# Values between keys and queries, the residual in quarters, inputs normalised a unit sooner, GpSimd's two copies swapped

## The reference, cut to what matters

```
xn = layernorm(x)
# branch 1: causal linear attention, 16 heads of 64
Q = elu(xn @ Wq + bq) + 1;  K = elu(xn @ Wk + bk) + 1;  V = xn @ Wv + bv
KV_t = KV_(t-1) + k_t v_t^T;  Ks_t = Ks_(t-1) + k_t
o_t = (q_t KV_t) / (q_t . Ks_t + 1e-6);      attn = o @ Wo + bo
# branch 2: soft decision tree of depth 8
gate = sigmoid((xn @ tree_Wq^T) @ routers^T)           # 255 nodes
leaf_prob = product of gate or 1 - gate along each path # 256 leaves
tree = (leaf_prob @ leaf_values) @ Wout_w^T + Wout_b
out = x + attn + tree
```

## Time and profile before

| | us |
|---|---|
| median of 3 runs | 1218.85 |
| lowest, highest | 1218.16, 1219.29 |
| profiled execution | 1219.74 |
| its span, first to last instruction | 1218.0 |
| PE busy | 1161.8 (95%) |
| DVE busy | 836.1 (69%) |
| POOL busy | 804.3 (66%) |
| ACT busy | 681.0 (56%) |

### The profile page before, as it was taken

How to read it: one execution, slowest core, us unless ns; L and a number is a source line. 1 busy time by engine, 2 the same in 40 slices (tenths; PEclk the granted TensorE clock), 3 DMA queues, 4 the chain that set the end, 5 groups by cost and what they waited for, 6 DMA issues and landing times.

```text
span 1218.0 us, 48108 instructions
## 1 busy us (share of the span) xinstructions
PE 1161.8 (95%) x21233; PEld 996.0 (82%) x21233; DVE 836.1 (69%) x2186; ACT 681.0 (56%) x990; POOL 804.3 (66%) x951
## 2 busy tenths in 40 slices
PE   5899999999999999999999999999999999999986
PEld 4789788887878879778897888878788797888866
DVE  4775875858677585876858667585876758767482
ACT  3563674737557374673737547374673746647371
POOL 3586667667666676766667676676666667676571
PEclk9999999999999999999999999999999999999998
DMA  7143532525344252533524435252452625335251
GB/s 233 20 80 52 86 68 54 91 52 89 60 65 90 45 97 50 89 63 55 93 49 90 58 62 98 45 89 54 84 68 57 94 45 89 63 57 77 55 71 36
DMA packets 271298, 87.54 MB, mean 72 GB/s; under 512 B 250721, under 2 KB 269424, under 8 KB 271088
## 3 DMA queue, kind: packets, MB, share of 16 engines
q1 hardware_dynamic: 271088, 84.46, 39.0%
HBM read 14.43 MB, written 8.39 MB: 19 GB/s over the span
## 4 chain that ended last, share of the span: by engine, by line
PE 63%; DVE 18%; ACT 6%; DMA 5%; issue 4%; POOL 3%; SPq 1%; POOLq 0%; ACTq 0%; DVEq 0%
PE w_pair L811 17%; PE s_pair L811 11%; PE s_pair L826 9%; PE o_pair L826 9%; PE s_pair L893 5%; PE o_pair L947 4%; DVE snaps L732 4%; DVE qT L659 3%; PE o_pair L933 3%; DVE oT L697 3%; DVE v_aug L668 3%; DVE xn L645 2%; DMA k_turned<-k_planes 2%; PE kv_pair L906 2%; ACT ex L522 2%
## 5 line engine op out<-in xcount | busy, mean ns | idle before, releaser
L406 POOL TENSOR_SCALAR_AFFINE_SELECT aT<-aT 64x512 f32<-64x512 f32 x256 | 171.7, 671 | 264.6 <-ACT aT L562 254.9
L562 ACT ACTIVATE aT<-s_pair 128x512 f32<-128x512 f32 x128 | 76.5, 598 | 382.6 <-PE s_pair L893 382.6
L811 PE MATMUL w_pair<-xnT,wk 128*128 128x512 f32 x768 | 212.1, 411 | 2.2 <-ACT k_tok L535 2.2
L811 PE MATMUL s_pair<-xnT,wq 128*128 128x512 f32 x756 | 201.1, 401 | 0.6 <-DVE o_tok L709 0.3
L732 DVE TENSOR_TENSOR snaps<-kv_pair,snaps 128x65 f32<-128x65 f32 x768 | 173.4, 226 | 26.4
L467 POOL COPY k_tok<-k_turned 128x1024 uint16<-128x1024 uint16 x126 | 171.4, 1361 | 22.7 <-POOL ffn_tok L459 14.6
L811 PE MATMUL w_pair<-wv,xnT 128*128 128x512 f32 x654 | 170.0, 395 | 0.0
L525 ACT ACTIVATE ex<-ex 128x512 f32<-128x512 f32 x256 | 161.9, 633 | 8.1
L449 POOL COPY k_planes<-kT 128x1024 uint16<-128x1024 uint16 x126 | 132.7, 1053 | 49.2 <-issue 26.5
L811 PEld LDWEIGHTS w_pair<-xnT,wk 128*128 128x128 f32 x768 | 134.3, 188 | 34.4 <-ACT k_tok L535 2.7
L811 PEld LDWEIGHTS s_pair<-xnT,wq 128*128 128x128 f32 x756 | 135.1, 188 | 27.0 <-DVE o_tok L709 2.4
(11 more groups left out here) (117 smaller groups left out, 2076.6 us busy)
## 6 DMA issues: line engine op xcount, KB each, us to landing
x_in<-in_L_attn_x_dram SPq DMA_DIRECT2D x16, 256.0 KB, 3.1
x_in<-in_L_attn_x_dram SPq DMA_DIRECT2D x32, 128.0 KB, 3.2
out_dram<-y_buf SPq DMA_DIRECT2D x32, 128.0 KB, 1.7
out_dram<-y_buf SPq DMA_DIRECT2D x64, 64.0 KB, 2.3
k_turned<-k_planes SPq DMA_TRANSPOSE x126, 3.2
stage<-in_L_attn_Wv_dram SPq DMA_DIRECT2D x2, 512.0 KB, 7.8
stage<-in_L_attn_Wk_dram SPq DMA_DIRECT2D x2, 512.0 KB, 10.0
stage<-in_L_attn_Wq_dram SPq DMA_DIRECT2D x2, 512.0 KB, 12.2
```

The costliest lines, as they stand in the source:

```text
L406: pool.affine_select(out=part, in_=part, compare_op=ALU.is_ge, fill=0.0, base=0, pattern=[[0, 2 * CH], [1, D]], channel_multiplier=-1).the ...
L811: last = pe.matmul(dst, l, r, start=i == 0, stop=i == len(steps) - 1)
```

## The change: what it does

- **Fills.** In units 1 to 6 the V product becomes the head, between K and Q, and xT, leaf or gate becomes the tail, after Q. Unit 0 (V1 twice) and unit 7 stay. `values_first` is gone.
- **GpSimd.** The keys of unit n+2 are put together before the output of unit n is taken apart. The residual is added in four quarters of 128x256, in units 1, 3, 4 and 5. The inverse deviation of block g+2 is computed among the tree levels of unit 7 of block g.
- **Normalising.** Block g+2 is normalised on DVE in unit 7 of block g, right behind its statistics, instead of in unit 0 of block g+1.
- **Turned output.** The high part (ACT) comes right after K's passes, the low part (DVE, L697) after K and V and before Q, instead of last or after Q.
- **SP.** The block is loaded in unit 6 instead of unit 2.
- **PE's waits.** The waits for mask, norm, inputs and leaves move into the middle or before the last matmul of the fills.

```diff
--- before.py
+++ after.py
@@ -42,19 +42,20 @@
     keys = divmod(n + 3, PAIRS) if n + 3 < blocks * PAIRS else None
     queries = divmod(n + 2, PAIRS) if n + 2 < blocks * PAIRS else None
     more = g + 1 < blocks
+
     head, tail = [], []
     if p == 0:
         head, tail = [("V1", 0, g)], [("V1", 1, g)]
     if p in (1, 2):
-        tail = [("V1", p + 1, g)]
+        head = [("V1", p + 1, g)]
         if more:
-            head = [("xT", p - 1, g + 1)]
+            tail = [("xT", p - 1, g + 1)]
+    if 3 <= p < PAIRS - 1 and more:
+        head = [("V0", p - 3, g + 1)]
     if p in (3, 4):
-        head = [("leaf", p - 3, g)]
-        if more:
-            tail = [("V0", p - 3, g + 1)]
+        tail = [("leaf", p - 3, g)]
     if p in (5, 6) and more:
-        head, tail = [("gate", p - 5, g + 1)], [("V0", p - 3, g + 1)]
+        tail = [("gate", p - 5, g + 1)]
 
 
     fills = [(("K", keys[1], keys[0]), W0)] if keys else []
@@ -363,8 +364,8 @@
                     turn_output(n)
                 if n + 3 < UNITS:
                     turn_keys(n + 3)
-                if p == 2 and g + 2 < BLOCKS:
-                    sp.wait_ge(x_consumed, g + 1)
+                if p == 6 and g + 2 < BLOCKS:
+                    sp.wait_ge(x_consumed, CH * (g + 1))
                     load_block(g + 2)
             store(BLOCKS - 1)
             sp.wait_ge(y_stored, STORES * BLOCKS)
@@ -407,13 +408,12 @@
                                        pattern=[[0, 2 * CH], [1, D]], channel_multiplier=-1).then_inc(a_masked, 1)
                 pool.wait_ge(a_masked, 2 * n + 2)
 
-            def residual(g):
+            def residual(g, c):
                 if g:
                     pool.wait_ge(y_stored, STORES * g)
                 pool.wait_ge(x_loaded[g % 2], LOADS * (g // 2 + 1))
-                pool.tensor_tensor(y_buf[:, :, :], x_in[:, g % 2],
-                                   y_bias[:, 0].unsqueeze(1).to_broadcast([P, CH, hid]), ALU.add)\
-                    .then_inc(x_consumed, 1)
+                pool.tensor_tensor(y_buf[:, c], x_in[:, g % 2, c], y_bias[:, 0], ALU.add).then_inc(x_consumed, 1)
+                pool.wait_ge(x_consumed, CH * g + c + 1)
 
             def gates(g):
                 for i in range(2):
@@ -438,6 +438,7 @@
                 pool.wait_ge(leaf_step, g * LEVEL_STEPS + 2 * l + 2)
                 pool.tensor_tensor(left, src[:, :, 0:n], right, ALU.subtract).then_inc(leaf_step, 1)
 
+            RESIDUAL_AT = (1, 3, 4, 5)
             FIRST_LEVELS = {0: range(0, 5), 1: range(5, 7), 2: range(7, depth)}
 
             def take_apart(m):
@@ -477,20 +478,19 @@
             take_apart(2)
             for n in range(UNITS):
                 g, p = divmod(n, PAIRS)
-                if p == 0 and g + 1 < BLOCKS:
-                    inverse_deviation(g + 1)
-                    pool.wait_ge(rstd_ready, 2 * g + 4)
+                if n == 0:
+                    inverse_deviation(1)
+                    pool.wait_ge(rstd_ready, 4)
                 if n + 1 < UNITS:
                     mask(n + 1)
+                if n + 2 < UNITS:
+                    put_together(n + 2)
                 if by_dma(n):
                     take_output_apart(n)
-                if n + 2 < UNITS:
-                    put_together(n + 2)
                 if n + 3 < UNITS:
                     take_apart(n + 3)
-                if p == 1:
-                    residual(g)
-                    pool.wait_ge(x_consumed, g + 1)
+                if p in RESIDUAL_AT:
+                    residual(g, RESIDUAL_AT.index(p))
                 if n in FIRST_LEVELS:
                     for l in FIRST_LEVELS[n]:
                         level(l, 0)
@@ -500,6 +500,10 @@
 
                     pool.wait_ge(o_turned_in, 16 * units_by_dma(n))
                     for l in range(depth):
+                        if l == 4 and g + 2 < BLOCKS:
+
+                            inverse_deviation(g + 2)
+                            pool.wait_ge(rstd_ready, 2 * g + 6)
                         level(l, g + 1)
                     pool.wait_ge(leaf_step, (g + 2) * LEVEL_STEPS)
 
@@ -605,15 +609,12 @@
                     put_output_together(n - 1)
                 for name, _ in unit_fills(n // PAIRS, n % PAIRS, BLOCKS):
                     kind, i, g = name
+                    if turned and kind != "K":
+                        high_of_turned(n - 1)
+                        turned = False
                     if kind in "KQ":
                         exponential(name)
-                        if kind == "Q" and turned:
-                            high_of_turned(n - 1)
-                            turned = False
                     elif kind == "oT":
-                        if turned:
-                            high_of_turned(n - 1)
-                            turned = False
                         high_of_output(name)
                     elif kind == "xT":
                         high(name, xnT[:, g % 2, 0, i])
@@ -641,6 +642,9 @@
                 if g == 1:
 
                     dve.wait_ge(filled[bank_of["tree", 1, 0]], count_of["tree", 1, 0])
+                if g > 1:
+
+                    dve.wait_ge(o_whole, units_by_dma((g - 1) * PAIRS - 2))
                 for c in range(CH):
                     last = dve.tensor_scalar(xn[:, c], x_in[:, g % 2, c], mean_var[:, c, 0:1], rstd[:, c:c + 1],
                                              ALU.subtract, ALU.mult)
@@ -669,14 +673,6 @@
                                   bv_all[:, half * n:(half + 1) * n].rearrange("p (h e) -> p h e", e=D), ALU.add)\
                    .then_inc(drained[bank_of[name]], 1)
 
-            def values_first(fills, p):
-
-                if p not in (2, PAIRS - 2):
-                    return fills
-                return [f for f in fills if f[0] not in ("Q", "V0", "V1", "oT", "kT")] + \
-                    [f for f in fills if f[0] in ("V0", "V1")] + \
-                    [f for f in fills if f[0] in ("Q", "oT", "kT")]
-
             def low_of_output(name):
                 _, p, g = name
                 dve.wait_ge(oT_hi, g * PAIRS + p + 1)
@@ -685,7 +681,7 @@
 
             def output(name):
                 i = name[1]
-                dve.wait_ge(x_consumed, name[2] + 1)
+                dve.wait_ge(x_consumed, CH * (name[2] + 1))
                 dve.wait_ge(filled[bank_of[name]], count_of[name])
                 dve.tensor_tensor(y_buf[:, 2 * i:2 * i + 2], psum_of(name).rearrange("p (c d) -> p c d", d=hid),
                                   y_buf[:, 2 * i:2 * i + 2], ALU.add)\
@@ -767,21 +763,21 @@
                 norm(n)
                 if n + 1 < UNITS:
                     carry(n + 1)
-                if p == 0 and g + 1 < BLOCKS:
-                    normalise(g + 1)
-                fills = [name for name, _ in unit_fills(g, p, BLOCKS)]
+                if n == 0:
+                    normalise(1)
                 turned = n and by_dma(n - 1)
-                for name in values_first(fills, p):
+                for name, _ in unit_fills(g, p, BLOCKS):
                     kind, i, b = name
+                    if turned and kind not in ("K", "V0", "V1"):
+                        low_of_turned(n - 1)
+                        turned = False
                     if kind in "KQ":
                         phi(name)
                     elif kind == "oT":
-                        if turned:
-                            low_of_turned(n - 1)
-                            turned = False
                         low_of_output(name)
                         if p == PAIRS - 1 and g + 2 < BLOCKS:
                             layer_norm(g + 2)
+                            normalise(g + 2)
                     elif kind in ("V0", "V1"):
                         values(name)
                     elif kind == "xT":
@@ -1051,13 +1049,18 @@
                 def normed():
                     until(o_normed, n + 1)
 
-                def head_ready():
-
+                def tail_ready():
                     for kind, i, g in (f for f, _ in fills):
                         if kind == "xT":
                             until(xn_ready, g + 1)
-                        if kind == "leaf" and i == 0:
+                        if kind == "leaf":
                             until(leaf_step, (g + 1) * LEVEL_STEPS)
+
+                def inputs_ready():
+                    for kind, i, g in (f for f, _ in fills):
+                        if kind == "V0" and i == 0:
+                            for t in range(KT_):
+                                until_drained(("xT", t, g))
 
                 def masked():
                     if n + 1 < UNITS:
@@ -1069,18 +1072,20 @@
                         until(s_copied, n + 2)
                     if kind in ("oT", "y"):
                         normed()
-                    if kind == "V0" and i == 0:
-                        for t in range(KT_):
-                            until_drained(("xT", t, g))
                     if kind == "leaf":
 
```

(23 more changed lines are left out.)

## The result

The changed kernel takes 1270.12 us (median of 4, 1263.3 to 1271.33) against 1218.57 for the kernel before (4 runs): a ratio of 1.0411, 95% interval 1.0373 to 1.0448. I had forecast 1234.5 and 1217 to 1244: the direction is right, the size is three times too small.

The account below looks back on a forecast made before the run. PE, busy 95%, was taken as the bound, so the change could only move its waits. Blocks of 74.39 against 73.375 gave +14.2 over 14, ends +1.5: +15.7, median 1234.5 us (+1.3%), range 1217 to 1244.

Parts of the forecast that it names:

- The floor of 7.71: Intervals p=1 to 6: scores to first ACT pass over Q 5.53, then 2.18 to next scores, at least 7.71 us.
- the floor I gave (73.73): Lowest block time forecast, all six intervals at 7.71 or 7.77 us: 73.73 us a block, 1225 us in total.
- the 74.39 of the forecast: New block: 19.55 for p=7, 7.80 for p=0, six intervals of 7.84; against 73.375 before, +1.015 us.
- The race of L697 and keys apart: DVE's L697 probably held by GpSimd's copy, two chances in three; qT 0.2 us late, intervals 7.90, taken as 7.84.
- The removed waits: PE waits that go: 0.6 us at p=0, 1.3 at p=2, 0.5 at p=6, at most 0.88 in some p=7.
- the 42 I gave as all that could be won: PE's waits inside the blocks, 3.0 us a block in the mean over 14 blocks: 42 us.
- Normalising, inverse deviation and block load in p=7: Work moved to or wanted in p=7, put at no cost: DVE idles 6.27 us there, the unit has 19.5.
- Rival 4: Move to p=7 is late; PE waits there 0.5 to 1 us a block: 1242 to 1249, chance 0.05.
- rival 3: L697 loses twice, to keys apart and the residual's quarter at p=1, 3, 4, 0.6 us each: 1260, chance 0.06.
- The ends: Cost outside the regular blocks: +0.6 us in the last block, +0.9 in the first.
- together, apart: GpSimd puts keys together before taking the output apart: output's transposition 1.4 us later, cost 0, 0 to 0.3 for some.
- my rivals: Cover is enough (0.11), gains and losses cancel (0.07), L697 loses twice (0.06), move to p=7 late (0.05).

Follow-up runs that it names:

- e1b: The changed kernel with GpSimd taking the output apart first and putting the keys together behind it, as before: 1232.9 us, ratio 1.0114.
- e4b: The changed kernel with the old fill order in p=1 to 4 and the output taken apart first: 1188.7 us, ratio 0.9755 to the kernel before.
- e9: e4b with the turned output's high and low parts ahead of Q in p=7 alone: 1182.12 us, ratio 0.9689 to the kernel before.
- e6: The kernel before with only the residual in quarters (p=1, 3, 4, 5) and the block load in p=6: 1205.86 us.
- e8: The kernel before with only V between K and Q and the gates behind Q in p=5 and 6: 1210.58 us.
- e2b: The kernel before with only GpSimd's copies swapped, keys put together first and output taken apart behind: 1295.74 us, ratio 1.0629.
- e3b: The changed kernel with the fill order of before in p=1 to 4, swap of GpSimd's copies kept: 1280.47 us.
- e5: The changed kernel, swap kept, with ACT putting the turned output together behind K's passes, its high and low parts behind Q: 1262.7 us, ratio 1.0349.
- e10: e5 with the changed kernel's order kept in p=7 on ACT and DVE: 1269.12 us.

## Why the prediction was wrong, point by point

**The fill order, right.** The floor of 7.71 was read from two places of the trace before; e1b has 7.73 to 7.78 in p=1 to 4. Its block of 73.82 lies at the floor I gave (73.73), not at the 74.39 of the forecast. That its time of 1232.9 is near the 1234.5 I forecast for everything is luck: the 14 blocks are 8 us cheaper than forecast, and the stretches before and after them about as much dearer. Between e1b and e4b the fill order, with the place of the turned output's parts, is worth 44 us.

**The race of L697 and keys apart, right in kind, mis-sized.** Timeline of e1b, p=2 of block 8; L693 is the L697 of before:

```profile
663.95 1.04 POOL L450 COPY k_planes<-kT 128x1024 uint16<-128x1024 uint16 x1
663.98 1.55 DVE L693 TENSOR_TENSOR oT<-o_full,oT 128x512 fp32r<-128x512 f32 x1
...
664.79 0.63 ACT L529 ACTIVATE ex<-ex 128x512 f32<-128x512 f32 x1
...
665.46 0.75 DVE L663 SCALAR_TENSOR_TENSOR qT<-s_pair,bias_one,ex 128x512 f32<-128x512 f32 x1
```

GpSimd starts 0.03 earlier (I had 0.08) and the DVE's instruction is held: the rule that I cited from the Trainium skill (SBUF — State Buffer, Who interferes with whom) agrees with this row. But it ends 0.54 after the copy's end, not 0.68: I counted the instruction's whole length behind the hold, where rows 6 and 8 already had 0.55 and 0.54. And qT isn't late at all. It starts 1.38 after ACT's first pass over Q (664.08 in this run), the same as in rows 9 without a hold. The intervals of p=1 to 4 are 7.73 to 7.78, where I took 7.84: the hold happens and costs nothing.

**The removed waits, right**: 0.6 at p=0, 0.9 at p=2, 0.5 at p=6 and the 0.9 of p=7 in every fourth block (19.38 flat in e1b and e9, with 20.4 still present in e4b). At p=2 I had laid all of the 1.3 to the residual's hold; e6 shows that quarters give back 0.9 of it, and 0.5 stays in the old fill order, where DVE takes the values ahead of Q. Together the gains are worth 36 us (e9), of the 42 I gave as all that could be won.

**Normalising, inverse deviation and block load in p=7, right**: p=7 is 19.38 in e1b. Rival 4 did not happen, nor rival 3. Yet the signs I had given for them, intervals over 8.2 and a p=7 past 20, both came in the changed kernel, from another cause; only e1b, where both are gone, tells them apart.

**The ends, low.** In e1b the first block has 66.71 against 62.41. One microsecond of that is in the interval of p=0, which is 9.9 to 10.1 in every run but that of before, the unchanged unit 0 of e8 among them; 3.3 is the change, where I had 0.9. From the first to the last scores of the last block it is 1.2 more, where I had 0.6. The very first scores also start 2.4 us later in e1b's trace (40.2 against 37.9), but the changed kernel, which begins alike, has 38.0, so that isn't the change.

**The step that failed** is this one: "The order 'together, apart' delays the output's transposition by 1.4 and makes it close up with the keys'; ACT wants it only in the next unit, so 0, with 0 to 0.3 for some." The swap costs 37 us in the changed kernel (1270.1 less 1232.9), 77 alone, 92 in the old fill order (1280.5 less 1188.7). The 1.4 itself came out: the output's transposition is issued 5.4 us after the scores in the changed kernel (205.44 below, scores at 200.06), and 4.0 in e1b (662.49, scores at 658.49). What I put at nothing was what ACT waits for it (64 us), and with it what a late landing does and what the swap does to GpSimd itself. I did not close the loop. Keys together, the copies, the keys' transposition and keys together again is a circle that must be faster than a unit. With the output's copy inside it, the changed kernel shows (timeline, an undisturbed unit of block 2):

```profile
202.95 1.36 POOL L468 COPY k_tok<-k_turned 128x1024 uint16<-128x1024 uint16 x1
...
204.37 1.04 POOL L460 COPY ffn_tok<-o_tok 128x1024 uint16<-128x1024 uint16 x1
205.44 1.26 SPq L347 DMA_TRANSPOSE ffn_tok<-ffn_tok  x1
205.47 1.04 POOL L450 COPY k_planes<-kT 128x1024 uint16<-128x1024 uint16 x1
...
206.79 1.28 SPq L335 DMA_TRANSPOSE k_turned<-k_planes  x1
```

From keys together to the keys' issue 3.84. Of the 1.34 more than in e1b below, 1.1 is the output's copy in between; the rest is SP, which issues the output's transposition until 206.70, when the keys' copy has ended at 206.51. With a landing of 3.2 the circle takes 7.0 us, with one of 4.7 it takes 8.5. With the output first, e1b has (662.52 to 665.02):

```profile
662.52 1.37 POOL L468 COPY k_tok<-k_turned 128x1024 uint16<-128x1024 uint16 x1
...
665.02 1.23 SPq L335 DMA_TRANSPOSE k_turned<-k_planes  x1
```

2.50, so 5.7 and 7.2. The units take 7.75 in the changed kernel and 6.87 in the old fill order. So the circle of before and of e4b has slack, slightly overrun only by a late landing in a short unit; that of the changed kernel is overrun by a landing over 3.9; that of e2b and e3b is overrun even by one on time in the short units, 7.0 against 6.87, so it hardly recovers inside a block. The losses of 37, 77 and 92 us go with that.

The traces bear the circle out. From keys together to the keys' issue takes 2.5 us in the median with the output first and 3.8 with the keys first, in every run. And where the circle binds, GpSimd puts keys together as soon as they land, within 0.15 us. Of the 84 times in units p=0 to 5 of blocks 1 to 14 it does so 4 times in e1b, 28 in e4b, 29 in the kernel before, 46 in the changed kernel, 57 and 59 in e5 and e10, 71 in e2b and 70 in e3b.

What is shown and what is not: the order of the copies as the cause is shown by e1b to e4b, with either fill order and in both directions; ACT as the place where PE pays in p=1 to 6 by e5. The circle is worked out from rows and fits all of these, but no run changed its length alone, so how the loss splits between the circle, the output's own late transposition and the clock stays open.

Of my rivals none was this one. All four worried about places where the change moves work; this was a circle through an engine, a queue and a DMA, whose length the swap changed by 1.3 us.

**Where the 51.6 us are.** 14 blocks of 2.94 are 41.2, the first block 5.3, the last 4.9. Of the 41.2, the swap has 14 x 2.50 = 35.0, and the fill order less the gains 14 x 0.44 = 6.2.

## What to carry to other kernels

When a step is put ahead of another on an in-order engine, look for the circles that run through it (engine, queue, DMA and back) and add up their length with the late landing as well as the median; compare it with the period of the loop, not with the slack at each hand-over. Such a circle shows in the profile as waits for DMAs that come and go from block to block. And two losses on one such circle do not add: a slower period elsewhere gives it slack, so undoing the other loss alone need not make the kernel faster: e3b came out 10 us slower in the median, at the edge of the spread.

## What the runs showed of the hardware that was not expected

- **Landings come in two groups.** In the kernel before 154 of the 235 transpositions land within 3.35 us of their issue, 48 take 4.3 to 5.1, and only 33 lie between. Of the 235, 68 are late, and each of them has a packet of an instruction queue between 1.5 us before and 3 us after its issue; of the others 60% do. In the changed kernel 91 of 92 against 52%. The page lists these queues as q8, 166 packets for 2.72 MB, and q14, 45 small ones. In the stretch of the changed kernel's long wait (230 to 236 us, two transpositions issued) there is one of q8:

```profile
q8 instruction: 1, 0.02, 1.5%
...
k_turned<-k_planes SPq DMA_TRANSPOSE x1, 4.9
```

That the packet causes the delay is not shown by a run of its own. Nor is it settled why late landings grow from 51 in e1b to 128 in e3b. The two transpositions are then issued closer: in every kernel with the keys first 76 to 90 of them start within 1.6 us of the one before, and 92 to 128 land late; in every kernel with the output first none does, and 51 to 82 land late.

- **A wait of PE can cost twice.** After two waits, 1.45 us in front of L904 at 239.14 and 2.54 us in front of the scores at 242.60, the granted clock was 0.57 in the mean of 4 us, so mostly at its half level (1.2 GHz), and a scores group that takes 0.65 took 1.14. Over the whole span the clock is 0.991 against 0.997, and 0.982 in e2b and 0.976 in e3b. My estimate from these means and spans: 1269.6 us at 0.991 lack 11.4 us of full speed and 1218.0 at 0.997 lack 3.7, so the clock has at most 8 of the 51 us; in the same way at most 20 of the 77 in e2b, and at most 24 of the 92 between e4b (0.994) and e3b.
